# Three places a unit for side work in loops 0 and 2, and linear attention's last pieces moved into loop 2

## The chip, the cores and the metric

One core of a Trainium2 chip. The metric is the device time of the program in microseconds, the median of several runs. The profile is of one execution, and times inside it count from the start of its span.

## The reference, cut to what matters

x has 4 x 1024 tokens of 128 numbers, float32.

```python
x = x + 0.5 * ffn0(layernorm(x))          # token-shift mix: sigmoid(r) * (relu(k)**2 @ W_v)
x = x + attention(layernorm(x))           # rotary softmax attention, 16 heads of 8
x = x + 0.5 * ffn0(layernorm(x))
x = x + 0.5 * moe(layernorm(x))           # 8 experts, top 2, rms_norm inside, plus skip
x = x + linear_attention(layernorm(x))    # softplus q and k, causal, 16 heads
x = x + 0.5 * moe(layernorm(x))

def moe(x):
    xn = rms_norm(x, norm_scale)
    scores_topk, idx = top_k(xn @ w_router.T, 2)
    weights = softmax(scores_topk)
    u, gate = split(moe_linear(xn, idx, w_up))     # row i gets the weights of its expert
    down = moe_linear(u * silu(gate), idx, w_down)
    return sum(down * weights) + x
```

## The kernel before, in words

The tokens stand in 32 tiles of 128, in 8 groups of four tiles. Each of the two moe layers is computed in two halves of 16 tiles: a *round* r is one half of one layer (rounds 0 and 1 are the first layer, 2 and 3 the second). A round has a *route* and a *loop*. The route normalises the tokens, computes the router's scores, picks the top two experts, counts how many tokens each expert has, gives every copy of a token a slot in a table ordered by expert in HBM, and scatters the tokens into it (32 indirect transfers by GpSimd). The loop then goes over the 39 tiles of the table, two tiles to a unit, 20 units (`UNITS`) and three more steps for the pipeline to drain. Loop r+1 gathers the results of loop r by 32 indirect transfers.

The order of the stages is: start, attention, loop 0, loop 1, linear attention, loop 2, loop 3, and a last gather. Route 0 lies in attention, route 1 in attention and loop 0, route 2 in linear attention, route 3 in linear attention and loop 2.

In a loop, unit u on TensorE is: `turn(u)` (transpose the two gathered tiles, L1656, behind two loads of the expert's offset into a register), `up(u-1)` (L1666), `turn_hidden(u-2)` (L1678), `down(u-3)` (L1692). VectorE scales what `turn` gave (L1733) and multiplies the two halves of the hidden layer (`hidden`, L1740); ScalarE does silu (L1767) and two copies out of PSUM (L1773, L1780); SP loads the slots three units ahead (L1829) and stores the results (L1835). SP does not begin the loads of a loop before all 32 scatters of its route have landed.

Everything that isn't the loop itself is cut into *pieces*. A piece is a tuple such as `("rext", r, g)`; every engine goes through the same list and issues what it has in that piece, so that the piece's place in the list is its place in every engine's in-order queue. `plan_loop` (L457) gives every unit two places: the first between `turn` and `up`, the second between `up` and `turn_hidden`. At each place `turn_of` (L184) takes one piece from each of up to four works, but at most one piece that needs TensorE. The side pieces of a loop share PSUM bank 1.

The pieces that matter here:

- `div`, `turn`, `proj`, `stats` end the last half of attention's batch 3: each needs the piece before it (TensorE, then VectorE, then TensorE). `factors` and `mn` to `ms` are the last group of the second token-shift mix. `mt`, `mk`, `mr`, `mv` use TensorE; `md` is GpSimd alone, `mx` VectorE alone; `ms` is the statistics of the result.
- `rroot` (L1447 and the helper at L561) is 16 small VectorE instructions, one behind the other, that give the inverse roots for the tiles named; `rnorm` (L1463) one VectorE instruction per tile; `rext` (L597 by its helper) four transposes on TensorE that wait for `rnorm` of that group, and a copy by ScalarE (L1566); `rscore` (L1417) eight small matmuls and a copy (L1470).
- `rtop` (L1479 to L1489) is VectorE alone, twice; `rcount` is two matmuls (L1426, L1427) and VectorE; `rscan`, `rplace`, `roff` are VectorE alone; `rweight` ScalarE and VectorE. From `rplace` on the slots are known and the scatters (`scat`, L1601 on GpSimd) can start: one at each place, and all that are left at the last place of the last unit. GpSimd holds a scatter back until TensorE has reached the same place of the loop (`pool_follow`, L1797), as far as the loop has matmuls there.
- In linear attention the steps n run from 0 to 131. Each has a list `extra` for route pieces, taken from `routes`, a list in which `spread` (L258) leaves empty steps. `ldiv`, `lturn`, `lproj`, `lstats` end a group of it, again one behind the other, as in attention. Those of the last group, 7, are `k.l_left` (L449): every engine does them behind the last step, before loop 2.

## Time and profile before

| what | value |
|---|---|
| three runs | 1348.8, 1349.03, 1354.61 us; median 1349.03 |
| the profiled execution | 1345.49 us, its span 1343.5 us |
| busy in the span | TensorE 81%, ScalarE 60%, VectorE 49%, GpSimd 28% |
| chain that ended last | TensorE 53%, VectorE 20%, ScalarE 11%, issue 6%, GpSimd 3%, DMA 2% |
| mean granted clock of TensorE | 0.899 |

How to read it: PE is TensorE's matmuls, PEld its weight loads, DVE is VectorE, ACT ScalarE, POOL GpSimd, SPq SP's DMA queue. L1656 is line 1656 of the kernel. A granted clock of 1.00 is 2.4 GHz and one of 0.50 is 1.2 GHz; values between are means over a stretch with both. "issue" is time in which an engine waited for nothing that the profile shows. Loop 0 runs from 662.6 to about 757 us, loop 1 from 770.7 to about 850, linear attention to 1129, its last pieces to 1137, loop 2 to 1219.5, loop 3 from 1222.3 to 1293, the last gather to the end.

### The profile page before, as it was taken

The numbers are of one execution on the slowest core, as the hardware profiler recorded it, in microseconds if no ns is written. First come the engines' busy times: TensorE is split into PE (matmuls) and PEld (weight loads), VectorE is DVE, ScalarE is ACT, GpSimd is POOL, SyncE is SP. The second block draws the span as 40 slices with busy tenths as digits, with TensorE's granted clock in tenths as the row PEclk, the third lists the DMA queues.
The fourth block names the chain that finished last, engine by engine and source line by source line (L and its number), as shares of the span: only waits on it lengthen the run. The fifth ranks groups of instructions, "written<-read, shape, count | busy, mean of one in ns | idle before, by whom it ended". The sixth has DMA issues, their size and how long they took to land.

```text
span 1343.5 us, 20969 instructions
## 1 busy us (share of the span) xinstructions
PE 1084.8 (81%) x7616; PEld 504.0 (38%) x7616; DVE 657.9 (49%) x2060; ACT 807.0 (60%) x1164; POOL 376.6 (28%) x376
## 2 busy tenths in 40 slices
PE   3459899899999999999879399787887776898940
PEld 2332222222322321232256256444544344565630
DVE  5752554456355340433165157667666663633522
ACT  4328788688898899989735255644443331464520
POOL 2100111111110102333003643243331263155535
PEclk8679999899999999999999789889888686898975
DMA  4360450432036502100012233100000001143522
GB/s 139 57 96 1 65 90 1 71 57 27 1 56 96 155 1 76 54 15 30 13 40 85 81 87 93 31 17 17 12 14 1 15 33 38 50 118 99 141 66 66
DMA packets 83411, 74.07 MB, mean 55 GB/s; under 512 B 11248, under 2 KB 77680, under 8 KB 82416
## 3 DMA queue, kind: packets, MB, share of 16 engines
q1 hardware_dynamic: 73824, 55.06, 18.8%
q0 software_dynamic: 8192, 16.79, 4.3%
q8 instruction: 66, 1.08, 0.4%
q10 hardware_dynamic: 1296, 0.86, 0.2%
q14 instruction: 33, 0.27, 0.1%
HBM read 39.26 MB, written 33.42 MB: 54 GB/s over the span
## 4 chain that ended last, share of the span: by engine, by line
PE 53%; DVE 20%; ACT 11%; issue 6%; POOL 3%; DMA 2%; another core or an unknown queue 0%; SPq 0%; POOLq 0%; DVEq 0%; ACTq 0%
PE ps L994 11%; PE ps L1666 9%; ACT attn_probs L1257 8%; PE ps L979 6%; PE ps L1692 4%; PE ps L597 3%; PE ps L888 2%; PE ps L1969 2%; POOL moe_back L1611 2%; PE ps L1678 2%; PE ps L1893 1%; DVE lin_scores L2098 1%; PE ps L1656 1%; DVE stats L554 1%; PE ps L1982 1%
## 5 line engine op out<-in xcount | busy, mean ns | idle before, releaser
L1257 ACT ACTIVATE attn_probs<-ps 128x1024 f32<-128x1024 f32 x512 | 485.7, 1075 | 86.0 <-PE ps L979 85.8
L994 PE MATMUL ps<-attn_probs,attn_v 128*18 128x512 f32 x2048 | 273.9, 607 | 5.7 <-DVE room L1224 5.1
L979 PE MATMUL ps<-stack 50*128 50x512 bf16 x1024 | 167.1, 391 | 17.3 <-DMA stack<-row_maxima 11.4
L1601 POOL DMA_INDIRECT slots<-moe_xr,moe_slot x128 | 125.3, 979 | 196.3 <-ACT attn_probs L1257 81.1
L1611 POOL DMA_INDIRECT moe_back<-results,moe_slot x128 | 123.9, 968 | 110.7 <-PE ps L1656 46.8
L1666 PE MATMUL ps<-stack,lin_scores 128*128 x312 | 153.8, 616 | 0.0
L979 PEld LDWEIGHTS ps<-stack 50*128 50x128 bf16 x1024 | 34.1, 94 | 253.6 <-ACT attn_probs L1257 226.3
L1767 ACT ACTIVATE lin_scores<-ps 128x256 f32<-128x256 f32 x156 | 58.6, 382 | 107.0 <-PE ps L1666 101.8
L1740 DVE TENSOR_TENSOR lin_scores<-ps,lin_scores 128x256 f32<-128x256 f32 x156 | 59.0, 418 | 103.5 <-ACT lin_scores L1767 85.2
L1692 PE MATMUL ps<-stack,lin_scores 128*128 x624 | 85.6, 281 | 8.9 <-ACT lin_heads_out L1780 6.8
L1692 PEld LDWEIGHTS ps<-stack,lin_scores 128*128 128x128 f32 x624 | 77.7, 195 | 10.7 <-issue 10.5
L1295 POOL TENSOR_TENSOR room<-room 128x512 f32<-128x512 f32 x16 | 24.5, 1530 | 186.2 <-DVE room L1089 186.2
L1666 PEld LDWEIGHTS ps<-stack,lin_scores 128*128 128x128 f32 x312 | 55.6, 199 | 39.8 <-issue 39.8
L2098 DVE TENSOR_TENSOR lin_scores<-ps,c_causal 128x512 f32<-128x512 f32 x64 | 41.1, 683 | 49.5 <-PE ps L1969 46.8
L1733 DVE TENSOR_SCALAR lin_scores<-ps,c_norm_scale 128x256 f32<-128x256 f32 x80 | 37.8, 473 | 54.1 <-PE ps L1656 48.5
L994 PEld LDWEIGHTS ps<-attn_probs,attn_v 128*18 128x18 f32 x2048 | 34.9, 96 | 75.9 <-issue 46.8
L1089 DVE SCALAR_TENSOR_TENSOR room<-ps,c_attn_b,moe_xr 128x512 f32<-128x512 f32 x32 | 23.9, 748 | 79.9 <-PE ps L888 78.4
L2168 ACT ACTIVATE lin_scores<-ps 128x512 f32<-128x512 f32 x64 | 34.8, 594 | 45.8 <-PE ps L1969 45.5
L1656 PE MATMUL ps<-c_ident,moe_gathered 128*128 128x128 f32 x156 | 33.0, 294 | 30.7 <-DMA moe_gathered<-slots 18.7
L1773 ACT ACTIVATE lin_scores<-ps 128x512 f32<-128x512 f32 x80 | 46.8, 584 | 14.9 <-PE ps L1678 8.4
L1678 PEld LDWEIGHTS ps<-c_ident,lin_scores 128*128 128x128 f32 x312 | 39.0, 143 | 37.5 <-issue 36.3
L888 PE MATMUL ps<-room,c_qk_w 128*128 128x256 f32 x128 | 45.3, 458 | 9.2 <-DVE mix_xt L804 8.8
(237 smaller groups left out, 1567.6 us busy)
## 6 DMA issues: line engine op xcount, KB each, us to landing
stack<-qk_parts SPq DMA_DIRECT2D x48, 256.0 KB, 8.9
moe_gathered<-slots SPq DMA_DIRECT2D x76, 128.0 KB
results<-lin_heads_out SPq DMA_DIRECT2D x76, 128.0 KB
slots<-zeros SPq DMA_DIRECT2D x2, 2496.0 KB, 14.9
qk_parts<-moe_xr SPq DMA_DIRECT2D x32, 128.0 KB, 2.7
qk_parts<-moe_xr SPq DMA_DIRECT2D x16, 192.0 KB, 2.8
stack<-in_expert_w SPq DMA_DIRECT2D x1, 3072.0 KB
x<-in_x SPq DMA_DIRECT2D x8, 256.0 KB, 8.2
```

Of the source, the lines that this page charges most:

```text
L888: instruction = T.matmul(k.ps[:, bank, cols], w[:, 2 * qk + which, :], d.xt[:, half * BANK:(half + 1) * BANK][:, cols], start=True, stop=True)
L979: instruction = T.matmul(k.ps[:, SCORE_BANKS[i % 3][s], :], d.stack[b % 2][rows, 1, pair, kt * P:(kt + 1) * P], d.stack[b % 2][rows, 0, pa ...
L994: instruction = T.matmul(k.ps[32 * j:32 * j + STRIP, PV_BANK, :], d.v[:, b % 2, kt, first:first + STRIP], d.probs[:, n % A_PROBS, j * BANK ...
L1257: A.activation(d.probs[:, n % A_PROBS, 2 * e * BANK:2 * (e + 1) * BANK], k.ps[:, banks[0]:banks[1] + 1, :].rearrange("p a n -> p (a n)"), ...
L1601: G.indirect_dma_start(out=k.dram["slots"][half], out_offset=bass.IndirectOffsetOnAxis(ap=d.slot[:, s, at, c:c + 1], axis=0), in_=d.xr[:, ...
L1611: G.indirect_dma_start(out=k.back[:, at % RING, c, :], out_offset=None, in_=k.dram["results"][half], in_offset=bass.IndirectOffsetOnAxis(a ...
L1666: T.matmul(k.ps[:, bank, :], d.gt[:, u % NB, i, :], w[:, bass.ds(offset[u, i], 2 * HIDDEN)], start=True, stop=True).then_inc(k.full[bank], 1)
L1678: instruction = T.transpose(k.ps[:, bank, at:at + P], d.h[:, u % NB, i, c * P:(c + 1) * P], k.ident[:, :])
L1692: instruction = T.matmul(k.ps[:, bank, i * DIM:(i + 1) * DIM], d.ht[:, u % NB, i, c * P:(c + 1) * P], w[:, 2 * HIDDEN + c * DIM:][:, bass. ...
L1740: V.tensor_tensor(d.h[:, u % NB, i, :], k.ps[:, bank, 0:HIDDEN], d.silu[:, u % NB, i, :], ALU.mult).then_inc(k.free[bank], 1)
L1767: A.activation(d.silu[:, u % NB, i, :], k.ps[:, bank, HIDDEN:2 * HIDDEN], ACT_FN.Silu).then_inc(k.e_silu, 1)
L2098: V.tensor_tensor(d.scores[:, m % NS, :].rearrange("p (j t) -> p j t", j=HPG), k.ps[:, bank, :].rearrange("p (j t) -> p j t", j=HPG), caus ...
```

## The change

1. `plan_loop` gives each unit of loops 0 and 2 a third place, between `turn_hidden` and `down`. TensorE and ScalarE have it there; VectorE, SP and GpSimd run it right behind the second. Scatters are still put at the first and second place alone.
2. The route of round 1's second part (and of round 3's) is no longer one work of eight tiles. Group 2 is a work of its own (`route_group`), which in loop 0 begins behind `proj` and in linear attention is put into `routes` behind `lstats` of group 6. Group 3 and what follows it come behind `ms` (behind `lstats` of group 7), with an empty piece behind each `rnorm`, `rtop` and `rcount` (`spaced`).
3. `k.l_left` is not done before loop 2 any more: it is the first work of loop 2.

```diff
-    yield OTHER, ("rnorm", r, part)
+    yield OTHER, ("rnorm", r, part * TPB, (part + 1) * TPB)
...
+def route_group(r, g):
+
+    yield OTHER, ("rroot", r, g * TPG, (g + 1) * TPG)
+    yield OTHER, ("rnorm", r, g * TPG, (g + 1) * TPG)
+    yield PRODUCT, ("rext", r, g)
+    yield PRODUCT, ("rscore", r, g)
...
+def spaced(pieces):
+
+    out = []
+    for piece in pieces:
+        out += [piece] + [(OTHER, ("rest",))] * (piece[1][0] in ("rnorm", "rtop", "rcount"))
+    return out
...
+        if ("lstats", GROUPS - 2) in out:
+            routes += spread(route_group(3, HALF_GROUPS - 2))
...
-    k.l_left = [piece for work in works for _, piece in work] + scatters
-    fill(k.l_left)
+    assert not scatters
+    k.l_left = works
...
-    slots = [[] for _ in range(2 * (UNITS + 3))]
+    places = [[[] for _ in range(PLACES)] for _ in range(UNITS + 3)]
+    slots = [place for unit in places for place in unit[:2]]
...
-        works = [list(route_part(3, 1, TPB)) + list(route_slots(3))]
+        works = k.l_left
...
+    for n, out in enumerate(place for unit in places for place in unit) if r % 2 == 0 else ():
+        out += turn_of(works, 4)
+        if n % PLACES < 2:
+            out += scatters if n // PLACES == UNITS + 2 and n % PLACES else scatters[:1]
+            scatters = scatters[1:]
+        if ("stats", BATCH - 1, HALVES - 1) in out:
+            works.insert(0, [(OTHER, ("factors", TILES - TPG, TILES))] + list(side_mix(SIDE_MIXES - 1)))
+        if ("proj", BATCH - 1, HALVES - 1) in out:
+            works.append(list(route_group(1, HALF_GROUPS - 2)))
+        if ("ms", SIDE_MIXES - 1) in out:
+            assert not works
+            works.append(spaced(route_group(1, HALF_GROUPS - 1)) + spaced(route_slots(1)))
+        if ("lstats", GROUPS - 1) in out:
+            works.append(spaced(route_group(3, HALF_GROUPS - 1)) + spaced(route_slots(3)))
+        if ("rplace", r + 1) in out:
+            scatters = transfers("scat", r + 1)
...
@@ -1695,7 +1722,7 @@
-        first, second = k.e_plan[r][u]
+        first, second, third = k.e_plan[r][u]
...
@@ -1709,6 +1736,8 @@
             side(piece)
         if 0 <= u - 2 < UNITS:
             turn_hidden(u - 2)
+        for piece in third:
+            side(piece)
         if 0 <= u - 3 < UNITS:
             down(u - 3)
...
-        for piece in second:
+        for piece in second + third:
             side(piece)
...
-    for piece in k.l_left:
-        side(piece)
-        route(piece)
```

## Rows read from the trace of the kernel before

**Rows 1.** Stretches: length, busy PE, PEld, DVE, ACT, POOL; PEclk, DMA share, GB/s

```profile
755.20:770.70 15.50, 0.01 (x1) 0.00 (x0) 0.00 (x0) 0.28 (x1) 9.83 (x11) 0.50 0.21 65
...
770.70:776.40 5.70, 4.98 (x10) 2.44 (x11) 0.96 (x2) 0.56 (x2) 3.79 (x4) 0.50 0.48 135
...
679.50:684.00 4.50, 4.50 (x21) 2.95 (x21) 1.21 (x4) 1.75 (x4) 0.24 (x1) 0.75 0.21 58
...
695.00:700.80 5.80, 3.18 (x18) 1.99 (x16) 5.32 (x30) 1.86 (x5) 0.00 (x0) 1.00 0.33 91
...
1116.00:1119.40 3.40, 0.00 (x0) 0.00 (x0) 0.20 (x1) 0.60 (x1) 2.92 (x4) 0.89 0.15 49
...
1119.40:1125.00 5.60, 5.05 (x42) 3.47 (x42) 1.84 (x4) 1.40 (x3) 3.08 (x4) 0.50 0.11 38
...
1170.00:1210.00 40.00, 39.15 (x215) 26.87 (x214) 14.68 (x36) 24.01 (x59) 24.00 (x25) 1.00 0.39 113
```

**Rows 2.** Timeline, end of loop 0 (start, length, engine, what, idle before it)

```profile
747.39 0.96 POOL L1601 DMA_INDIRECT slots<-moe_xr,moe_slot  x1 [0.42 <-PE ps L1666]
...
756.99 0.28 ACT L1780 ACTIVATE lin_heads_out<-ps 128x128 f32<-128x128 f32 x1 [3.13 <-remote]
...
766.36 0.96 POOL L1601 DMA_INDIRECT slots<-moe_xr,moe_slot  x1 [0.30 <-issue]
...
768.60 3.21 SPq L1829 DMA_DIRECT2D moe_gathered<-slots  x5
```

**Rows 3.** TensorE's waits from 663 to 751 us (total, times, longest)

```profile
PE ps L597 <- DVE moe_xr L1463: 2.6, 1, 2.6
...
PE ps L597 <- DVE room L586: 2.3, 1, 2.3
...
PE ps L1426 <- DVE moe_both L1488: 1.7, 1, 1.7
...
PE ps L771 <- DVE mix_mixed_r L811: 1.1, 1, 1.1
```

**Rows 4.** Timeline, from linear attention into loop 2

```profile
1134.32 2.08 PE L1942 MATMUL ps<-c_lin_w,stack 128*128 128x128 f32 x8 [0.69 <-ACT stack L2150]
...
1144.15 1.12 PE L597 MATMUL ps<-c_ident,moe_xr 128*128 128x128 f32 x4 [3.19 <-DVE moe_xr L1463]
...
1145.06 3.62 PE L1666 MATMUL ps<-stack,lin_scores 128*128 x4
...
1152.44 0.95 PE L1417 MATMUL ps<-router_scaled,moe_xrt 128*128 128x8 f32 x8
...
1153.94 1.88 PE L1666 MATMUL ps<-stack,lin_scores 128*128 x4
...
1159.10 0.23 PE L1426 MATMUL ps<-moe_both,before_bf 128*128 128x128 bf16 x1 [1.73 <-DVE moe_both L1488]
```

**Rows 5.** Timeline, TensorE, two expert matmul groups one unit apart

```profile
1177.13 1.88 PE L1666 MATMUL ps<-stack,lin_scores 128*128 x4
...
1180.39 1.88 PE L1666 MATMUL ps<-stack,lin_scores 128*128 x4
```

**Rows 6.** Timeline, loop 0: its first matmuls and VectorE's side pieces

```profile
667.37 1.88 PE L1666 MATMUL ps<-stack,lin_scores 128*128 x4
...
667.57 0.69 DVE L1157 TENSOR_TENSOR x<-x,ps 128x512 f32<-128x512 f32 x1 [0.41 <-PE ps L946]
...
694.49 0.86 DVE L554 BATCH_NORM_STATS2 stats<-x 128x6 f32<-128x128 f32 x4
...
696.05 0.16 DVE L1452 TENSOR_SCALAR moe_root_var<-moments 128x8 f32<-128x8 f32 x1
...
698.97 0.75 DVE L1740 TENSOR_TENSOR lin_scores<-ps,lin_scores 128x256 f32<-128x256 f32 x2
...
699.64 2.13 DVE L1463 TENSOR_SCALAR moe_xr<-x,moments,moe_root 128x128 f32<-128x128 f32 x8
...
701.69 0.47 DVE L1733 TENSOR_SCALAR lin_scores<-ps,c_norm_scale 128x256 f32<-128x256 f32 x1
```

More of the change, by code:

```diff
@@ L1711, in pe_loop @@
             turn_hidden(u - 2)
+        for piece in third:
+            side(piece)
         if 0 <= u - 3 < UNITS:
@@ L1743, in dve_loop @@
     for u in range(UNITS + 3):
-        first, second = k.e_plan[r][u]
+        first, second, third = k.e_plan[r][u]
         if u < UNITS:
@@ L1792, in act_loop @@
             turn_hidden(u - 2)
+        for piece in third:
+            side(piece)
         if 0 <= u - 3 < UNITS:
@@ L1853, in sp_loop @@
             store(u - 3)
-        for piece in second:
+        for piece in second + third:
             side(piece)
@@ L2222, in pool_linear @@
             route(piece)
-    for piece in k.l_left:
-        side(piece)
-        route(piece)
 class Stage:
```

35 lines of the change are left out of this document (10 added, 25 removed).

## The prediction

> **What bounds the kernel now.** I read the chain that ended last, then the busy time by stretch, then the timeline where a stretch is thin. The chain is mostly TensorE, with a share for VectorE (the shares stand in the table of the profile), so I ask where TensorE stands still around the changed places. There are three. (a) After loop 0 it has nothing for 15.5 us, 755.2 to 770.7 [rows 1]. The timeline shows why [rows 2]: GpSimd issues scatters back to back, from 747.39 to 766.36, 16 of them, 18.97 / 15 = 1.265 us apart; the last ends at 767.32, SP's load of loop 1 starts 1.28 us later, TensorE 2.1 us behind that. ScalarE had finished loop 0 at 757.27. The scatters set the end of (a), not the loop. (b) In loop 0, pieces make TensorE wait for VectorE: 2.6, 2.3, 1.7 and 1.1 us [rows 3], 7.7 us together, and the clock is 0.75 over the 4.5 us behind the second of them [rows 1], some 1.1 us of full speed lost. (c) Between linear attention and loop 2 the chain of group 7 (ldiv, lturn, lproj) ends on TensorE at 1136.4, and the first expert matmuls start at 1145.06 [rows 4], since `rext` waits for VectorE's `rroot` and `rnorm` of eight tiles.
>
> **The scatters.** The positions follow from the generators. Before, `rplace` of route 1 lies in unit 12's first place; 20 scatters follow one by one and 12 pile up in the last place of unit 22. After: div 0.0, turn 0.1, proj 0.2; rest and rroot(group 2) 1.0; stats and rnorm 1.1; factors and rext 1.2; mn and rscore 2.0; mt 2.1, md 2.2, mx 3.0, mk 3.1, mr 3.2, mv 4.0, ms 4.1; rroot(group 3) 4.2, rnorm 5.0, rest, rext 5.2, rscore 6.0, rtop 6.1 and 7.0, rcount 7.2, rscan 8.1, rplace 8.2. Scatters run from 9.0, two per unit (2.53 us of GpSimd in a unit of 3.26 us, [rows 5]), and 5 are left for the last place. The last scatter that waits for the loop is that of 20.1 both times, and it is followed by 15 before (the row at 747.39 is it) and by 8 after. 7 x 1.265 = **8.9 us** off the gap. What is late next: ScalarE and SP end the loop at 757.3, so with the loads at 768.6 - 8.9 = 759.7 about 2 us are left until the loop's own end decides. TensorE still stands some 7 us there, longer than the 3.4 us of 1116.0 to 1119.4, behind which the clock was 0.50 [rows 1]; the restart stays at the lower level and I take no gain in it.
>
> **Loop 0's body.** All work of the pieces is kept, so only waits and clock count. Removed: the 7.7 us of waits and the 1.1 us of clock above. Added, by following TensorE and VectorE in order:
> rext(group 2) at 1.2 stands behind up(0), whose last matmul is issued at about 669.1 (667.37 + 1.88, less 0.2 of overlap with the next; [rows 6]). VectorE must by then have done the proj add (till about 667.9; before at 667.57 + 0.69, [rows 6]), turn(1) 0.5, rroot 2.9 (696.05 to 698.97; its cost is per instruction, so a half of the tiles costs the same), hidden(0) 0.75, stats 1.25, rnorm of four tiles 1.1 (half of 2.13) [rows 6]: 674.4. Wait: 5.3 us. The proj, which now has no turn(1) ahead of it, waits 0.8 for its copy (0.69, the copy being of the add's size). mk at 3.1 waits about 0.6 (VectorE does turn(3) 0.5 and the two mx after GpSimd's difference). rext(group 3) at 5.2: between ms and it VectorE has stats 1.25, rroot 2.9, turn(5) 0.5, rnorm 1.1, begun about 2 us after mv; TensorE has th, down, turn, up, th, some 4 us: it waits 3.2 us, where before it waited 2.6. rcount with its empty place waits no more. Sum added: 9.9 us of waits against 7.7.
> The clock: a wait of 5.3 us is longer than that stand of 3.4 too; back at work on loop matmuls it needs about 6 us (0.50 over 770.7 to 776.4, 4.98 us busy) [rows 1], so 2.5 us are lost; behind the 3.2 us wait the same may happen or not (over 695.0 to 700.8, with a 2.6 us wait in it, it stayed 1.00): I take 0.8, bounds 0 and 2.5. So loop 0's body is (9.9 - 7.7) + (3.3 - 1.1) = **4.4 us longer**. Bounds: no clock loss and a first wait hidden down to the 2.6 us of the old one, 4.9 us better; both stretches at the low level in full and 2 us more waiting, 4 us worse.
> The Trainium skill (TensorE: Matmul & The Clock Gate, Part 1) says that the warm-up is a budget of time and not a number of matmuls. By that rule each of the two waits would cost the same 2.5 us, 1.7 more than my sum; the row with clock 1.00 behind the 2.6 us wait speaks for a smaller second one.
>
> **VectorE and GpSimd.** Four rroots in place of two: 2.9 us more of VectorE in loop 0 and as much in linear attention. Priced in the waits above in loop 0; in linear attention it falls at steps 121 to 123, where TensorE stands 3.4 us anyway [rows 1]: nothing. If that stand went, up to 2.9 us would show. GpSimd's proj additions lie ahead of the first scatter and hold nothing up; SP gets no new piece, its stores come ahead of the second and third places as before.
>
> **Linear attention into loop 2.** Two pieces, rext and rscore of group 6, move into steps 126 and 128, on the path: 1.12 us for the turn [rows 4] and about 1.8 for the scores (0.95 at full clock [rows 4], the level there being 0.50 [rows 1]): +2.9. turn(0) now goes ahead of ldiv, +0.4. So lproj ends at 1136.4 + 3.3 = 1139.7 (2.08 us of it from 1134.32, [rows 4]). Then turn(1) and up(0) at once, the latter 3.6 at the low level [rows 4], till 1143.5: the first expert work stands 5 us ahead of before. But rext(group 3) at 2.2 waits: silu 0.5, hidden 0.75, stats 1.25, rroot 2.9, turn(2) 0.5, rnorm 1.1 bring VectorE to 1150.6, TensorE having run out (up(1), th(0)) at about 1146.5. Then turn(3), rscore, and up(2) starts at 1153.0 at full clock, 1154.2 at the low level, against 1153.94 before [rows 4]. At the low level 1.3 more is lost behind it. The rcount wait of 1.73 [rows 4] goes. Together between -2.6 and -0.1; after 4 us of standing I take the latter: **0.1 us**. Scatters of route 3 end one later behind the loop's last paced one (1.265 us); the last store and load hide it.
>
> **The sum.** -8.9 + 4.4 - 0.1 = -4.6 us. The profiled execution took 1345.5 us around a span of 1343.5, so 1340.9 for it; it is 3.5 below the median of the runs shown, 1349.0, to which the same difference gives **1344.4 us**.
>
> **The rivals.** *The new waits are cheap.* If the clock keeps its higher level behind the 3.2 and the 4 us waits (as over 695.0 to 700.8), and some of VectorE's work slips into gaps that my order does not see, loop 0's body is even or 1 us longer and loop 2 brings 2.6: -8.9 + 1 - 2.6 = -10.5, 1338.5 us. For it: the change's empty places are cut just for that. Against: the first wait has no empty place. *The waits take all.* Both low stretches in full (+1.7), 2 us more of waiting at the first, and a late instruction stretch such as that at 1116.0 once more, some 1 us: about 1349, no change. *Slower: the clock stays low.* Over 1119.4 to 1125.0 TensorE was busy 5.05 of 5.6 us and still had 0.50 [rows 1], so being busy does not by itself bring it back. If from the first wait (674.4) it stayed at that level for the seven units that still hold pieces, 7 x 3.26 = 23 us of work at full speed would take 23 us more, less 3.8 of the later waits that vanish and 3.3 counted: +15.9, so 1360.3. It decides at the first expert matmuls behind rext(group 2): clock 0.5 beyond 6 us. The Trainium skill (same page, Part 4, PE-mode transpose) states that transposes do not count as busy in the same way; by that rule the pieces, of which rext and mt are transposes, would favour this case. Against it: the steady loop, whose every unit has two sets of transposes, is granted the full clock, 1.00 over 1170 to 1210 [rows 1]. *No effect in place:* VectorE runs the third place right behind the second, so for it only the spacing changes; where its work ends last, as in both first waits, the third place gives nothing. That is inside the forecast.
>
> **How the numbers follow.** Forecast (-2 to -6.7) 0.45; cheap waits 0.35; the waits take all 0.12; slower 0.08. The range holds the forecast, the no-change case and most of the cheap one: 1336 to 1350. A measurement of this kernel tells about 0.5%, 6.7 us, from no change. Faster by more than that: the cheap case with a little of the forecast's edge, 0.38; within it 0.54; slower 0.08.
>
> **What would show it.** Right: 8 scatters behind the last that waits for TensorE in loop 0, the load of loop 1 1.3 us behind them; a wait of TensorE for `moe_xr` of about 5 us near 670 to 674 and one of about 3 near 697; a clock near 0.5 for some us behind the first; loop 2's first expert matmuls about 5 us earlier, and a wait of about 4 us two units on. Wrong: no such waits (cheap case), or loop 0's last scatters hidden behind its own end (then less than 8.9 is to be had), or units at half clock till unit 7.

## The result, and the profile after

| kernel | median, us | ratio to before |
|---|---|---|
| before, 20 runs | 1348.91 (1343.91 to 1354.61) | |
| after, 20 runs | 1352.95 (1349.22 to 1356.52) | 1.0030, 95% 1.0019 to 1.0041 |

The change makes the kernel 4.0 us slower (1352.95 - 1348.91). The forecast was 1344.4 in 1336 to 1350: the loss is small, inside the 0.5% named there, but the time lies outside the range and on the other side of before.

**Loop 0's waits** came as the prediction had them, but for two. TensorE's waits from 659 to 751 us in the trace of after, where before had [rows 3] (waited for, us in total, times, longest):

```profile
PE ps L624 <- DVE moe_xr L1490: 8.6, 2, 5.4
...
PE ps L798 <- DVE mix_mixed_r L838: 1.7, 1, 1.7
PE ps L1453 <- DVE moe_both L1515: 1.7, 1, 1.7
...
PE ps L1683 <- DVE lin_scores L1762: 0.9, 1, 0.9
PE ps L973 <- DVE room L1179: 0.9, 1, 0.9
```

The 8.6 us are rext(group 2), 5.4 where 5.3 was forecast, and rext(group 3), 3.2. mk waits 1.7 instead of 0.6, and rcount still 1.7 instead of nothing.

**The gap behind loop 0**, against [rows 2], in the timeline of after (start, busy time, engine, line, what; idle time before it and what ended it):

```profile
755.47 0.95 POOL L1628 DMA_INDIRECT slots<-moe_xr,moe_slot  x1 [0.42 <-PE ps L1693]
...
758.72 0.38 ACT L1809 ACTIVATE lin_heads_out<-ps 128x256 f32<-128x256 f32 x1 [2.27 <-remote]
...
760.87 0.38 ACT L1802 ACTIVATE lin_scores<-ps 128x256 f32<-128x256 f32 x1 [1.76 <-issue]
...
765.14 0.38 ACT L1809 ACTIVATE lin_heads_out<-ps 128x256 f32<-128x256 f32 x1 [3.88 <-remote]
765.57 0.95 POOL L1628 DMA_INDIRECT slots<-moe_xr,moe_slot  x1 [0.30 <-issue]
...
765.66 1.22 PE L1719 MATMUL ps<-stack,lin_scores 128*128 x4 [5.26 <-issue]
...
768.71 0.28 ACT L1809 ACTIVATE lin_heads_out<-ps 128x128 f32<-128x128 f32 x1 [3.19 <-remote]
769.44 3.24 SPq L1860 DMA_DIRECT2D moe_gathered<-slots  x5
...
771.60 0.69 PE L1683 MATMUL ps<-c_ident,moe_gathered 128*128 128x128 f32 x2 [4.73 <-DMA moe_gathered<-slots]
```

Eight scatters behind one that is paced by TensorE, as counted; the last ends at 766.52. But the load comes at 769.44, not 1.3 us behind it: ScalarE's last copy of the loop ends at 768.99. From the paced scatter to that copy it is 13.5 us, against 9.9 (747.39 to 757.27) before [rows 2]. TensorE and ScalarE stand in this tail for 1.8 to 5.3 us at a time, marked "remote" or "issue": the trace names no instruction of this core for which they wait.

**From linear attention to loop 2**, against [rows 4], the timeline of TensorE after:

```profile
1139.06 2.05 PE L1973 MATMUL ps<-c_lin_w,stack 128*128 128x128 f32 x8 [0.78 <-ACT stack L2175]
...
1141.32 2.96 PE L1693 MATMUL ps<-stack,lin_scores 128*128 x4
...
1144.34 1.88 PE L1693 MATMUL ps<-stack,lin_scores 128*128 x4
...
1151.11 1.12 PE L624 MATMUL ps<-c_ident,moe_xr 128*128 128x128 f32 x4 [4.45 <-DVE moe_xr L1490]
...
1153.01 1.85 PE L1444 MATMUL ps<-router_scaled,moe_xrt 128*128 128x8 f32 x8
...
1154.71 3.76 PE L1693 MATMUL ps<-stack,lin_scores 128*128 x4
...
1160.92 1.88 PE L1693 MATMUL ps<-stack,lin_scores 128*128 x4
...
1163.89 0.23 PE L1453 MATMUL ps<-moe_both,before_bf 128*128 128x128 bf16 x1 [0.65 <-DVE moe_both L1515]
...
1166.03 0.41 PE L1683 MATMUL ps<-c_ident,moe_gathered 128*128 128x128 f32 x2 [0.78 <-issue]
```

The first expert matmuls start at 1141.32 instead of 1145.06. Five us later TensorE waits 4.45 us for `rnorm` of group 3, as worked out, and is then at the lower clock for ten us. The rows from 1160.92 on come behind that: up(3), `rcount`, which waits 0.65 us (1.73 before), and the next `turn`. Of the next rows the upper is the stretch behind loop 0's first wait, the lower the one behind 1151.11 (stretch, busy PE, PEld, DVE, ACT, POOL; PEclk, DMA share, GB/s):

```profile
675.00:679.00 4.00, 4.00 (x11) 2.45 (x12) 1.56 (x6) 0.38 (x1) 0.00 (x0) 0.50 0.11 33
1151.10:1161.00 9.90, 9.61 (x33) 6.86 (x34) 3.24 (x11) 2.06 (x5) 0.00 (x0) 0.52 0.00 0
```

Landmarks of all traces that follow, read off their timelines. Loop 0 counts from its first `turn`: the last `up`, the last copy by ScalarE, the end of the last scatter, the first `turn` of loop 1. The rest counts from linear attention's first copy of its sums: the last such copy, loop 2's first and last `up`, loop 3's first `turn`.

| trace | up(19) | copy | scatter | loop 1 | lin. end | up(0) | up(19) | loop 3 |
|---|---|---|---|---|---|---|---|---|
| before | 83.5 | 94.7 | 104.8 | 108.2 | 261.3 | 277.1 | 345.1 | 354.3 |
| after | 95.0 | 109.8 | 107.3 | 112.4 | 264.8 | 272.4 | 349.3 | 360.4 |
| after_again | 92.6 | 98.3 | 105.0 | 108.4 | 259.3 | 265.7 | 340.8 | 349.3 |
| loop0_only | 92.8 | 98.5 | 105.2 | 108.7 | 252.4 | 265.9 | 331.7 | 340.2 |
| loop2_only | 84.0 | 89.7 | 105.2 | 108.7 | 259.5 | 265.9 | 341.1 | 349.6 |
| loop0_only_2 | 94.0 | 105.9 | 106.4 | 110.0 | 261.3 | 277.1 | 344.9 | 354.1 |
| loop2_only_2 | 85.0 | 96.9 | 106.2 | 109.5 | 261.7 | 269.7 | 346.3 | 357.0 |

One thing is needed to read it. The kernels ran on several chips, in sessions of two kinds: before takes 1344 to 1349 us in those of the first kind and 1329 to 1331 in those of the second. The first two and the last two rows are from the first kind, the three between from the second. A ratio is always to before in the same session; it is estimated over all runs and differs a little from the ratio of the medians. What makes the kind is not known: the expectations speak of chips, but the chip numbered 6 stands in both kinds (before at 1329.9 in one session, at 1348.5 in another), and whether that is the same chip is not on record. Of before there is a trace of the first kind alone; for the second, the half of loop0_only and of loop2_only that is left as it was stands for it.

### The profile page after: what moved, and what is told of

Same layout as the page of the kernel before. It is cut to its first block, busy times and chain, and to the rows that moved or that the text cites. A ratio compares the mean times of both kernels' runs of the same rounds, so it can differ in the third digit from the quotient of the medians.

```text
span 1351.1 us, 20959 instructions
## 1 busy us (share of the span) xinstructions
PE 1081.6 (80%) x7573; PEld 509.4 (38%) x7616; DVE 664.2 (49%) x2092; ACT 806.6 (60%) x1164; POOL 376.0 (28%) x376
## 4 chain that ended last, share of the span: by engine, by line
PE 51%; DVE 20%; ACT 12%; issue 5%; POOL 3%; another core or an unknown queue 2%; DMA 2%; SPq 0%; POOLq 0%; DVEq 0%; ACTq 0%
PE ps L1021 11%; ACT attn_probs L1284 8%; PE ps L1693 8%; PE ps L1006 6%; PE ps L1719 4%; PE ps L624 3%; PE ps L915 2%; POOL moe_back L1638 2%; PE ps L2000 2%; PE ps L1705 2%; PE ps L1683 1%; PE ps L1924 1%; DVE lin_scores L2126 1%; PE ps L1960 1%
## 5 line engine op out<-in xcount | busy, mean ns | idle before, releaser
L1693 PE MATMUL ps<-stack,lin_scores 128*128 x312 | 157.6, 629 | 0.0
L1719 PE MATMUL ps<-stack,lin_scores 128*128 x624 | 85.9, 281 | 13.5 <-issue 9.9
L915 PE MATMUL ps<-room,c_qk_w 128*128 128x256 f32 x128 | 43.6, 441 | 11.2 <-DVE mix_xt L831 8.8
L1809 ACT ACTIVATE lin_heads_out<-ps 128x256 f32<-128x256 f32 x80 | 30.2, 377 | 37.3 <-PE ps L1719 24.7
```

The costliest lines, as they stand in the source:

```text
L915: instruction = T.matmul(k.ps[:, bank, cols], w[:, 2 * qk + which, :], d.xt[:, half * BANK:(half + 1) * BANK][:, cols], start=True, stop=True)
L1693: T.matmul(k.ps[:, bank, :], d.gt[:, u % NB, i, :], w[:, bass.ds(offset[u, i], 2 * HIDDEN)], start=True, stop=True).then_inc(k.full[bank], 1)
L1719: instruction = T.matmul(k.ps[:, bank, i * DIM:(i + 1) * DIM], d.ht[:, u % NB, i, c * P:(c + 1) * P], w[:, 2 * HIDDEN + c * DIM:][:, bass. ...
```

## Experiments

### Which half loses the time

`loop0_only` takes the change in loop 0 alone, `loop2_only` that in linear attention and loop 2 alone, `after_again` both.

```diff
 loop0_only: loop 2's works and k.l_left as before
-        works = k.l_left
+        works = [list(route_part(3, 1, TPB)) + list(route_slots(3))]
...
 loop2_only: loop 0's works as before, at the first two places
-            works.append(spaced(route_group(1, HALF_GROUPS - 1)) + spaced(route_slots(1)))
+            works.append(list(route_part(1, 1, TPB)) + list(route_slots(1)))
...
```

> The change in loop 0 alone; linear attention, its last pieces and loop 2 are as before. Theory A (the traces of before and after add up: in loop 0 the body grew by 11.5 us and the gap behind it shrank by 7.2, in linear attention and loop 2 another 6 us were lost): this one is 0 to 4 us slower than before, 1349 to 1353 us, and the part between the first turn of loop 0 and the first of loop 1 is 112 us instead of 108. Theory B (all of the loss is loop 0's, loop 2's part gives some back): 5 to 7 us slower, 1354 to 1356. My prediction on record had -4.5, 1344.4.

> The other half alone: loop 0 as before; group 6 of route 3 in linear attention, the last pieces in loop 2 with three places. Theory A: 3 to 6 us slower than before, 1352 to 1355: linear attention ends 3.5 us later, and the first expert matmuls of loop 2 come 4 us earlier but a wait of 4 to 5 us for moe_xr with a half clock behind it takes that back. Theory B: 1 to 3 us faster, 1346 to 1348. My prediction on record had -0.1, 1348.9.

> The changed kernel unchanged, to see which stalls of its trace come back. If the late signals of TensorE at 1180 to 1182.5 (three engines wait for it together) and in loop 0's tail (ScalarE late by 2.3, 1.8, 3.9 and 3.2 us) belong to the kernel, they stand at the same instructions again, to 0.5 us. If they belong to one execution, they are somewhere else. Time 1352 to 1354.

Measured, with before at 1329.1: loop0_only 1332.1, 1.0015 (0.9994 to 1.0036); loop2_only 1339.9, 1.0079 (1.0054 to 1.0104); after_again 1341.3, 1.0079 (1.0049 to 1.0108). In a session with before at 1344.5 the two halves were run again:

> The same kernel as loop0_only. On a chip with before at 1330 it was 1.0015 of it: a body 8.6 us longer and a gap 8.9 us shorter. On a chip with before at 1349 the tail of the loop was 11.2 us long in the trace of before and 14.8 in that of after, against 5.7 there, and decides the gap. Theory T (this tail takes the gain of the scatters): 4 to 7 us over before there, 1.003 to 1.005. Theory N (the long tail of after was one execution): 0 to 2 us over, 1.000 to 1.002.

> The same kernel as loop2_only: 1.0079 of before on a chip with before at 1330, where linear attention runs at the full clock up to its end. On a chip with before at 1349 the trace of before has a stand of 3.4 us and the lower clock behind it at that place, so that the added wait and the clock behind it cost little. Theory T: 0 to 3 us over before there, below 1.002. Theory N: 1.005 to 1.008 on either.

loop0_only_2 1345.5, 1.0002 (0.9988 to 1.0016); loop2_only_2 1349.2, 1.0032 (1.0016 to 1.0047).

So on both kinds the loss is that of linear attention and loop 2, and loop 0's half is not told from no change. Theory A's 3 to 6 us for loop 2's half fit the first kind (4.3, from the ratio 1.0032) and are too low for the second (10.5, from 1.0079); its 112 us for loop 0 did not come. B fell. Of the second pair of expectations N was right for loop 0: the long tail does not cost it its gain. For loop 2's half 1.0032 lies between T and N. The traces agree: loop 0 with its gap takes 108.4 and 108.7 with the change, 108.7 without (after_again, loop0_only, loop2_only); from the first copy of the sums to loop 3 it is 349.3 and 349.6 with the change and 340.2 without, 9.3 us. In the session of loop2_only_2 that is 357.0 against 354.1, 2.9 us.

after_again does not show the stalls in loop 0's tail: its last copy is 5.7 us behind the last `up`, as in all traces of the second kind (5.6 or 5.7), where the paced kernels of the first have 11.1 to 14.8, before among them; `hold_tail`, below, has 6.3. Nor does it show the late signals at 1182.5, which come back in loop2_only_2, of the first kind (4.9 us from up(8) to up(9), 3.3 in after_again). They go with the kind of session.

### What loop 2's half loses

In the trace of loop0_only, loop 2 starts as before, without the stand of [rows 1] at 1116.0. What linear attention calls groups 6 and 7 are groups 2 and 3 of round 3. TensorE's timeline in loop0_only:

```profile
1126.03 0.44 PE L1680 MATMUL ps<-c_ident,moe_gathered 128*128 128x128 f32 x2 [1.39 <-DMA moe_gathered<-slots]
1128.54 0.66 PE L1680 MATMUL ps<-c_ident,moe_gathered 128*128 128x128 f32 x2 [2.07 <-DVE lin_scores L1759]
1132.39 1.12 PE L621 MATMUL ps<-c_ident,moe_xr 128*128 128x128 f32 x4 [3.20 <-DVE moe_xr L1487]
```

and in after_again, with the windows of its two low stretches there (columns as above):

```profile
1115.62 1.11 PE L624 MATMUL ps<-c_ident,moe_xr 128*128 128x128 f32 x4 [1.92 <-DVE moe_xr L1490]
...
1124.03 0.69 PE L1683 MATMUL ps<-c_ident,moe_gathered 128*128 128x128 f32 x2 [0.20 <-DMA moe_gathered<-slots]
...
1130.35 2.91 PE L1693 MATMUL ps<-stack,lin_scores 128*128 x4
...
1140.08 1.11 PE L624 MATMUL ps<-c_ident,moe_xr 128*128 128x128 f32 x4 [4.44 <-DVE moe_xr L1490]
...
1143.67 3.76 PE L1693 MATMUL ps<-stack,lin_scores 128*128 x4
```

```profile
1115.60:1125.00 9.40, 9.18 (x75) 7.19 (x76) 2.60 (x8) 1.79 (x3) 3.46 (x4) 0.50 0.26 81
1139.40:1149.40 10.00, 9.01 (x29) 6.29 (x30) 3.41 (x12) 1.96 (x4) 0.00 (x0) 0.50 0.01 2
```

Three things are seen. The moved `rext` of group 6 waits 1.92 us for VectorE, and behind it TensorE has the clock 0.50 for 9.4 us, with 9.18 busy: linear attention ends 6.9 us later than in loop0_only (259.3 - 252.4). Loop 2's first `turn` waits for its load in both, which SP issues when route 2's scatters have landed (in loop0_only the last ends at 1122.66, the load is issued at 1123.93); up(0) is at 265.7 and 265.9. And rext(group 3) waits 4.44 us, with ten us at 0.50 behind it; loop 2 takes 75.1 us from its first to its last `up` instead of 65.8.

Where those 9.3 us lie is told by the starts of single `up`s, counted as in the table above:

| trace | up(2) | up(3) | up(4) | up(9) | up(19) |
|---|---|---|---|---|---|
| before | 285.9 | 291.2 | 294.6 | 312.4 | 345.1 |
| after | 285.8 | 292.0 | 297.3 | 317.0 | 349.3 |
| loop0_only | 273.9 | 279.1 | 282.5 | 299.3 | 331.7 |
| after_again | 279.0 | 285.2 | 290.5 | 308.4 | 340.8 |
| warm (below) | 278.7 | 283.4 | 289.8 | 307.7 | 340.0 |

Up to up(2) after_again has lost 5.2 us against loop0_only; on the first kind the earlier start pays for that, and after is level with before. Behind up(2) both lose about 4 us more (4.2 and 4.0). Of these 0.9 come up to up(3), with the clock low. 2.0 come up to up(4), where the clock is back at 1.00 and where `rcount` now lies: in before it waits 1.73 us ahead of up(3), in after 0.65 us ahead of up(4), and the `turn` behind it stands another 0.78 (the rows at 1163.89 and 1166.03 above). The unit with `rcount` in it takes 5.4 us in after and 5.3 in before, so nothing was saved there. The last 1.1 to 1.4 are smaller stands in the units behind.

`warm` keeps TensorE busy in the four waits for `rext`, with matmuls into the bank that the rext overwrites:

```diff
+            for _ in range({(1, 2): 5, (1, 3): 3, (3, 2): 2, (3, 3): 4}.get((r, g), 0)):
+                bank, n = k.use[piece]
+                T.wait_ge(k.free[bank], n)
+                T.matmul(k.ps[:, bank, :], k.ident[:, :], k.expert_w.rearrange("p e c -> p (e c)")[:, 0:4 * P],
+                         start=True, stop=True)
             T.wait_ge(k.e_xr, HALF_GROUPS * r + g + 1)
```

> The changed kernel, with 5, 3, 2 and 4 idle matmuls of 128x512 (0.94 us each) ahead of the four rext that wait for VectorE (5.2, 3.1, 1.9 and 4.4 us), into the PSUM bank that the rext then overwrites; the output is the same. The waits stay, only TensorE is not idle in them. Theory C (half of the loss is the clock behind the waits: in the trace of after it is 0.50 over the 9.4 us behind the rext in linear attention and some 10 us behind the one in loop 2, and 0.57 to 0.66 over 10 us in loop 0, some 13 us lost at the lower level): 9 to 13 us less than after, about the time of before or up to 3 us below it. Theory W (the waits themselves are the loss, the clock comes back as late either way, or falls for another reason): within 2 us of after, that is 0.6 to 0.8% over before.

Measured 1335.3, 1.0041 (1.0022 to 1.0060), with before at 1329.9: 5 us less than after_again (0.0038 x 1330). Its windows, and three rows of TensorE in loop 2:

```profile
672.00:682.00 10.00, 7.93 (x37) 4.45 (x35) 8.08 (x37) 2.22 (x5) 0.74 (x1) 1.00 0.04 13
1113.00:1120.00 7.00, 6.23 (x75) 4.25 (x70) 4.54 (x17) 1.18 (x2) 5.40 (x6) 1.00 0.15 49
1120.00:1130.00 10.00, 5.87 (x47) 5.10 (x36) 1.03 (x3) 2.48 (x3) 0.00 (x0) 0.59 0.24 72
1137.00:1145.00 8.00, 6.21 (x23) 3.43 (x22) 4.19 (x18) 0.60 (x1) 0.00 (x0) 0.84 0.01 2
```

```profile
1123.20 0.69 PE L1688 MATMUL ps<-c_ident,moe_gathered 128*128 128x128 f32 x2 [2.58 <-DMA moe_gathered<-slots]
...
1140.18 0.66 PE L624 MATMUL ps<-c_ident,moe_xr 128*128 128x128 f32 x4 [1.01 <-DVE moe_xr L1495]
...
1151.72 0.23 PE L1458 MATMUL ps<-moe_both,before_bf 128*128 128x128 bf16 x1 [1.71 <-DVE moe_both L1520]
```

The clock stays 1.00 through loop 0's waits and to the end of linear attention. Then loop 2's first `turn` waits 2.6 us for its load, which the earlier end had uncovered, and the clock goes all the same. So theory C is right in kind, the clock behind the waits costs time, but 5 us and not 9 to 13. And most of the 5 us are not where the change loses: loop 0 with its gap takes 105.2 us instead of 108.4, and from the first copy of the sums to loop 3 it is 348.5 instead of 349.3. In loop 2 up(3) follows up(2) after 4.8 us instead of 6.2, the clock being higher, but then `rcount` waits 1.71 us for VectorE's `moe_both` instead of 0.67, and up(4) follows after 6.4 us instead of 5.3. There the gain of the clock is handed on to the next wait for VectorE. (One trace each.)

`group6_loop2` does group 6 in loop 2, at unit 0.0 and 1.1:

```diff
-        if ("lstats", GROUPS - 2) in out:
-            routes += spread(route_group(3, HALF_GROUPS - 2))
-        works = k.l_left
+        works = k.l_left + [rested(route_group(3, HALF_GROUPS - 2), 2)]
```

> The changed kernel, but group 6 of route 3 is not done inside linear attention: its rroot lies at unit 0.0 of loop 2, its rext at 1.1. Theory L (moving it into linear attention costs 6.9 us: a wait of 1.9, the turn and the scores, and the lower clock for the 9.4 us behind it): linear attention ends 6.9 us earlier; loop 2 gets a wait of 2 to 4 us more at unit 1 and takes some of it back: 2 to 5 us less than after. Theory 0 (it falls into time in which TensorE stands anyway, as my prediction has it): no less than after, or 2 to 4 us more for what loop 2 has to do in addition.

Measured 1340.0, 1.0082 (1.0051 to 1.0114). Linear attention is 7 us shorter and nothing is gained:

```profile
1124.91 0.69 PE L1689 MATMUL ps<-c_ident,moe_gathered 128*128 128x128 f32 x2 [6.42 <-DMA moe_gathered<-slots]
...
1125.87 1.76 PE L1966 MATMUL ps<-c_head_rows,lin_sums 128*128 128x36 f32 x8
...
1132.53 2.60 PE L1699 MATMUL ps<-stack,lin_scores 128*128 x4
```

`turn(0)` now stands 6.42 us ahead of the last pieces of linear attention, which need nothing from it. Theory L had the 6.9 us right and missed where they go. That is a fact that my prediction lacked: **loop 2 cannot start before route 2's scatters are through**. On the second kind, where linear attention ends sooner, a few us saved or lost on TensorE before that are hidden behind them: turn(0) comes at 258.6, 259.4 and 258.6 in loop0_only, after_again and group6_loop2. In the traces of before and after it does not wait for its load: it comes at 268.2 and 264.8, 10.5 and 5.8 us behind SP's issue.

`no_second_root` leaves the added inverse roots out (14 VectorE instructions, twice; the roots of an earlier round serve instead):

```diff
+            if (r, piece[2]) not in ((1, 2 * TPG), (3, 2 * TPG)):
                 V.tensor_scalar(var[:, 0, :], moments[:, :, 1], LN_EPS, None, ALU.add)
...
```

> The changed kernel without the inverse roots of group 2 in round 1 and of group 6 in round 3 (the 14 small VectorE instructions of the added rroot; its last two, the keep factors, stay); the roots of an earlier round are used for these tiles, so that the routing differs. Theory V (VectorE is what TensorE waits for at all these points, and the second rroot of 2.9 us is the added work): each of the two gets 2.5 us shorter, the wait of 5.2 us in loop 0 falls to 2.7 and that of 1.9 in linear attention goes, with some of the clock behind them: 3 to 8 us less than after, 0.2 to 0.5% over before. Theory P (the places are wrong, a wait of this length is hidden or taken by the next one): within 2 us of after, 0.6 to 0.8% over before.

Measured 1340.7, 1.0068 (1.0043 to 1.0092), against 1.0079 of after_again: not told apart. The wait of 5.2 us became 4.3, that of 4.4 stayed, that of 1.9 in linear attention went, with its low clock, and `turn(0)` waits 4.9 us for the load instead. VectorE now waits 1.69 us for ScalarE's silu. The chain from `proj` through the unit to `rnorm` is long even without the roots. Theory V's 3 to 8 us did not come in the traces (0.7 us less in loop 0, 0.3 more behind it), as P has it; the intervals alone do not rule out 3.

`rests` puts more empty places behind three rnorm: 4 for group 2 in loop 0 and 3 for the last group in loop 2 (`rested` does it), and three empty steps for group 6 in linear attention (not shown):

```diff
-            works.append(list(route_group(1, HALF_GROUPS - 2)))
+            works.append(rested(route_group(1, HALF_GROUPS - 2), 4))
...
-            works.append(spaced(route_group(3, HALF_GROUPS - 1)) + spaced(route_slots(3)))
+            works.append(rested(route_group(3, HALF_GROUPS - 1), 4) + spaced(route_slots(3)))
```

> The changed kernel with empty places in front of the rext that wait: 4 more in loop 0 for group 2, three steps in linear attention for group 6, 3 more in loop 2 for group 3. The waits of 5.2, 1.9 and 4.4 us should go, that of 3.1 stays; loop 2's scatters come one unit later (two more behind its end, 2.5 us, hidden or not). Theory W+C (waits and the clock behind them are the whole loss): 5.2 + 1.9 + 4.4 = 11.5 us of waits and some 10 of clock, less 8 for work of VectorE that still has to be waited for elsewhere (before had 3.2 + 2.1 us at this point in loop 2, and 2.4 in loop 0): 8 to 14 us less than after, 0 to 4 us below before. Theory D (VectorE has too much to do there, every piece only passes its wait to the next): less than 3 us below after.

Measured 1336.3, 1.0042 (1.0024 to 1.0060), 5 us below after_again, less than the 8 to 14 of theory W+C. The three waits went. In their place `mt` in loop 0 waits 7.0 us for VectorE (2.4 in loop2_only), and `turn` in loop 2 3.5 us for VectorE's scaling of the unit before. Here too the gain is loop 0's: 105.3 us with its gap. Loop 2's last `up` comes 2.6 us sooner than in after_again (338.2), but loop 3 only 0.4 (348.9), for its load again waits for scatters, which now end later. As theory D has it, part of a wait is passed on: VectorE has its 4 us of `rroot` and `rnorm` to do in the first units, and every engine's queue is in order.

### Other arrangements

`one_part` has one rroot of eight tiles in loop 0 (with three places), and of group 6 only VectorE's part in linear attention; `one_part_unpaced` also lets the scatters run free:

```diff
 one_part, loop 0
-            works.append(spaced(route_group(1, HALF_GROUPS - 1)) + spaced(route_slots(1)))
+            works.append(rested(route_part(1, 1, TPB), 2) + spaced(route_slots(1)))
...
 one_part_unpaced
-                if piece[0] in ("gath", "scat"):
+                if piece[0] == "gath":
                     pool_follow(G, k, r, u, second)
```

> Three places a unit as in the changed kernel, but in loop 0 the route of round 1 has one rroot and one rnorm of eight tiles again, with two empty places behind; scatters start at unit 10 instead of 9 (12 before). Linear attention's last pieces are done before loop 2 again; of group 6 only rroot and rnorm (VectorE alone) lie in linear attention, its rext is loop 2's first piece, and group 7's rroot comes at unit 1. If my reading of the losses is right (loop 0: the second rroot makes the body longer; linear attention: the turn, the scores and the clock behind them on TensorE; loop 2: the wait of 4.4 us and the clock behind it): loop 0's body is 2 to 4 us longer than before instead of 8.6 and the gap 6.3 shorter, 2 to 4 us gained; the first expert matmuls of loop 2 start some 5 us earlier than before and 3 to 4 us of that are kept: 4 to 8 us below before. If the third place or the order in itself costs: no better than before.

> The kernel one_part, and GpSimd issues the scatters without holding each back until TensorE is at its place. If the last scatters set the gap behind loop 0 there (10 behind the last paced one, 11.4 us): back to back they end some 3 us earlier, and the gap is shorter by that until the loop's own end decides: 2 to 4 us below one_part. If back-to-back scatters beside the loop slow it (their DMA traffic, or late signals as in the tail of the trace of after), it is not below one_part.

Measured: one_part 1331.1, 1.0004 (0.9982 to 1.0025); one_part_unpaced 1324.5, **0.9946** (0.9923 to 0.9968), with before at 1331.1. one_part is no faster, where 4 to 8 us were expected: it starts loop 2's experts 2.9 us earlier than loop0_only (263.0 against 265.9) and has lost 4.7 by its last `up`; loop 0 with its gap is 107.5, against 108.7. Earlier starts are again given back in the next units. Without the pacing loop 0 takes 102.6.

`loop0_one_part` is loop 0 of one_part with the rest as before:

> Loop 0 as in one_part (three places, one rroot of eight tiles, scatters from unit 10, held back as before), linear attention and loop 2 as before. In the trace of one_part loop 0 with its gap took 107.5 us against 108.2 to 108.7 with loop 0 as before, and the rest is before's: 1 us below before, 0.999, within the interval of no change on either kind of chip. If the loss of loop 0's second rroot is larger than the traces show: 0.996 to 0.998. If the long tail of a chip with before at 1345 takes the gain (10 scatters instead of 15 beside it, the tail at 11 us): 1.000 to 1.001.

1344.2, 0.9989 (0.9970 to 1.0007), with before at 1345.5: no difference that can be told.

### What scatters do to the engines beside them

`after_unpaced`, `before_unpaced` and `best` (loop 0 of one_part_unpaced, the rest as before) take the pacing away as above; `hold_tail` does the opposite in the kernel before:

```diff
+                if piece[0] == "scat" and u > UNITS:
+                    bank, n = k.use["edown", r, UNITS - 1]
+                    G.wait_ge(k.free[bank], n + 1)
```

> The changed kernel, but GpSimd does not hold a scatter back until TensorE is at the same place: 32 scatters run back to back from 719.8, 40.5 us, to 760.3, instead of 766.5. Theory 1 (scatters running back to back beside the draining loop are what makes its tail slow: 13.5 us from the last paced scatter to the last copy, 9.9 before): only some four lie in the tail, it is 4 to 7 us shorter, loads of loop 1 at 762 to 765, in loop 2 a few us as well: 1343 to 1348. Theory 2 (the tail is slow by itself): loads stay at 769, time as after, 1352 to 1354. Theory 3 (back-to-back scatters slow TensorE's signals wherever they run): the units from 9 on get longer, more than 3.3 us each, and it is slower than after, 1355 to 1360.

1335.4, 1.0036 (1.0016 to 1.0057), before at 1329.1: 6 us less than after_again, the amount of theory 1. The reason of theory 1 is not seen: the tail is 5.7 us in both, the scatters end 40.1 us behind the start of the first, and loop 1 starts 2.6 us earlier (105.8 against 108.4); the rest is not located in the two traces.

> The kernel before, and GpSimd issues the scatters of loops 0 and 2 without holding each back until TensorE is at its place; nothing else is changed. In the trace of before they start at 723.4 and end at 767.3, 43.9 us for 32; back to back they need 40.5. If the scatters alone set the gap behind loop 0: 3.4 us less, and loop 2, whose scatters end before its last copy, gains nothing: 3 to 4 us below before, ratio 0.997. If what helps in the unpaced kernels is something else (places in which GpSimd's wait holds back others), more than that; if the traffic of unpaced scatters slows the loop, 0 to 3 us above before.

> Loop 0 as in one_part_unpaced (three places, one rroot of eight tiles, scatters from unit 10, not held back), linear attention and loop 2 as before. The part from the first turn of loop 0 to that of loop 1 was 102.6 us in one_part_unpaced and 108.2 before: 5.6 us gained; the part from linear attention's first copy of the sums to loop 3 was 342.7 there and 340.2 with loop 2 as before: another 2.5 us. Sum: 8 us below before, ratio 0.994; at least as fast as one_part_unpaced (0.9946). If loop 2's part of one_part_unpaced is no loss (the two traces are one execution each), it is 0.9946 to 0.997.

> The same kernel as before_unpaced, once more. Theory S (scatters that are not held back delay TensorE's signals to the other engines, 4 to 10 us each in the trace of before_unpaced, but only on some chips: those on which before takes 1349, not those on which it takes 1330): on a chip with before at 1349 again 1.03 to 1.04 of it, on one with before at 1330 it is 0.997 to 1.000. Theory K (it is this kernel's own, whatever the chip): 1.03 to 1.04 on either.

before_unpaced 1397.2, **1.0360** (1.0332 to 1.0388), best 1405.0, **1.0424** (1.0402 to 1.0446), both with before at 1348.5; before_unpaced_2 1395.9, 1.0390 (1.0360 to 1.0421), before at 1344.5. I had expected 0.994 to 1.003 for the first two; of the third, S and K both had 1.03 to 1.04 in a session of this kind, so it does not tell them apart. ScalarE's waits from 726 to 768 us, beside the scatters, in before_unpaced, and in one_part_unpaced with before at 1331:

```profile
ACT lin_scores L1773 <- remote: 13.7, 2, 10.1
ACT lin_heads_out L1780 <- remote: 12.9, 2, 9.9
ACT lin_scores L1767 <- remote: 9.7, 2, 5.1
```

```profile
ACT lin_scores L1802 <- PE ps L1699: 5.6, 9, 1.2
ACT lin_heads_out L1815 <- PE ps L1725: 4.8, 12, 1.1
```

and what that leaves of 34 us beside 28 scatters, first before_unpaced, then one_part_unpaced:

```profile
727.00:761.00 34.00, 10.59 (x41) 5.77 (x39) 1.99 (x5) 4.47 (x11) 25.77 (x28) 0.69 0.21 67
```

```profile
727.00:761.00 34.00, 30.42 (x171) 21.25 (x171) 10.21 (x25) 21.19 (x55) 25.77 (x28) 1.00 0.39 115
```

The scatters are the same, 28 with 25.77 us of GpSimd; TensorE gets 10.6 us of matmuls done in the one, 30.4 in the other. The longest stands of TensorE and VectorE in loop 0 of before_unpaced:

```profile
757.91 1.12 PE L1678 MATMUL ps<-c_ident,lin_scores 128*128 128x128 f32 x4 [15.58 <-issue]
...
767.82 0.48 DVE L1733 TENSOR_SCALAR lin_scores<-ps,c_norm_scale 128x256 f32<-128x256 f32 x1 [19.88 <-remote]
```

Expected of hold_tail:

> The kernel before, but the 15 scatters behind that of 20.1 in loop 0 (and the few in loop 2) are held back until ScalarE's last copy of the loop. No scatter runs beside the draining loop. Theory S: the tail, from the last up to the last copy, is 5.7 us and not 11.2, on any chip; the gap behind it is 15 scatters long, so that the whole is 0 to 4 us slower than before. Theory I (late instructions of ScalarE and TensorE, whatever GpSimd does): the tail is 9 to 12 us on a chip with before at 1349, and the whole 5 to 8 us slower.

1355.0, 1.0068 (1.0044 to 1.0092), before at 1344.5. With no scatter beside the draining loop, ScalarE's last copies come as TensorE's matmuls end:

```profile
749.87 0.38 ACT L1780 ACTIVATE lin_heads_out<-ps 128x256 f32<-128x256 f32 x1 [0.97 <-PE ps L1692]
...
751.58 0.38 ACT L1780 ACTIVATE lin_heads_out<-ps 128x256 f32<-128x256 f32 x1 [1.05 <-PE ps L1692]
752.85 0.28 ACT L1780 ACTIVATE lin_heads_out<-ps 128x128 f32<-128x128 f32 x1 [0.88 <-PE ps L1692]
```

The last copy ends 5.0 us behind the paced scatter at 748.11, against 9.9 before [rows 2] and 13.5 after, and 6.3 us behind the last `up`. So theory S holds for the tail: the scatters issued back to back make it long, in sessions of the first kind (11.2 us before, 6.3 here). The whole is 9 us slower (0.0068 x 1344.5), more than the 0 to 4 expected. In the trace loop 0 with its gap is 4.8 us longer (113.0 against 108.2), since 15 scatters then follow; the rest lies behind it and is not explained: linear attention ends 3.7 us later (265.0) and loop 2's tail is 1.8 longer. What delays TensorE's signals was not tried; that it goes with the kind of session is shown only by one_part_unpaced and after_unpaced against the three others, and no unpaced kernel ran on both kinds.

## Why the prediction was wrong, point by point

**The scatters, -8.9 us.** Right, by the traces of the second kind. Eight follow the paced one, and without the long tail the gap is 15.8 us (108.4 - 92.6) instead of 24.7 (108.7 - 84.0). In the trace of the result the tail decides, which I had given 2 us of slack: I took its end from the trace of before, where it was already stretched, and let it move with the body alone. Over the 12 runs of loop0_only_2 this costs nothing that can be told (1.0002).

**Loop 0's body, +4.4 us.** Mis-sized: 8.6 (92.6 - 84.0). Waits at 5.2, 0.9 and 3.1 stand where 5.3, 0.8 and 3.2 were worked out (the 3.2 by luck: its terms add up to 3.75). The term "rcount with its empty place waits no more" is wrong, it waits 1.7; mk waits 1.7 for 0.6; two small ones, 0.9 and 0.3, were not seen. Up to up(19) TensorE stands 17.2 of 92.6 us in after_again and 11.2 of 84.0 in loop2_only: 6.0 more, where the sum had 2.2. It is busy 2.6 us longer (75.4 against 72.8), where the sum had 2.2 for the clock. So -8.9 and +8.6: loop 0 gives nothing.

**"In linear attention it falls at steps 121 to 123, where TensorE stands 3.4 us anyway: nothing."** That stand goes with the first kind: 3.6 us of "issue" again in loop0_only_2 and hold_tail, 5.0 in loop2_only_2, absent in loop0_only. Where it is absent, the added work waits 1.9 us and the clock is 0.50 behind it, +6.9 to the end of linear attention. I had named the condition ("if that stand went, up to 2.9 us would show") and not its clock. But these 6.9 us do not reach loop 2, which waits for its load.

**The first expert matmuls 5 us earlier.** Right for the first kind, that of the result: 4.7 and 7.4 us (277.1 to 272.4 and to 269.7). Nothing on the second (265.9 to 265.7), where turn(0) waits for its load.

**"At the low level 1.3 more is lost behind it. The rcount wait of 1.73 goes", "-0.1".** This is the step that failed. The wait of 4.2 us came at 4.45, and up(2) stood at 285.8 against 285.9 before, level as forecast. From there to the last `up` after loses 4.2 us. First, the clock: from up(2) to up(3) it takes 6.2 us, 2.9 more than the steady 3.27, where I had 1.3; the low stretch lasted 9.9 us with 9.61 busy at 0.52, 4.6 us lost in all, against the 2.5 priced for it. Second, the wait of `rcount` did not go. It is 0.65 us for VectorE and 0.78 at the `turn` behind it, and the unit takes 5.4 us where before's takes 5.3, so the 1.73 that I took off did not come; the same term was wrong in loop 0. `warm` shows that the clock is not what sets this: with a higher clock behind up(2), `rcount` waits 1.71. Third, some 1.4 us of small stands up to up(9), for which I had nothing. I followed the edit to the unit where both kernels stood level and closed the sum there with a wait taken off. In after the tail adds 1.7 (8.1 against 6.4 us from the last `up` to the last copy). The whole term is +2.9 us in loop2_only_2 and +6.1 in after, by the runs +4.3 (0.0032 x 1344.5, interval 2.2 to 6.3), in place of -0.1; on the second kind, where the earlier start is missing, 9.3 in the traces.

**The clock.** The prediction had 2.5 and 0.8 us behind loop 0's two waits for `rnorm`. Three windows of after_again, behind the wait of 5.2 us, behind that of 3.1, and behind `rcount` (1.7 us, and 0.7 at the next `turn`):

```profile
671.60:678.60 7.00, 6.54 (x18) 4.11 (x19) 3.59 (x20) 0.98 (x2) 0.00 (x0) 0.51 0.06 19
697.10:705.10 8.00, 7.54 (x44) 5.51 (x45) 3.63 (x12) 3.12 (x7) 0.00 (x0) 1.00 0.16 43
709.10:714.10 5.00, 4.51 (x16) 2.71 (x17) 1.24 (x4) 1.44 (x4) 0.00 (x0) 0.66 0.21 56
```

So some 3.2 us are lost behind the first, nothing behind the second, and 1.5 behind `rcount`, where I had none; busy time times the missing share of the clock gives these. By the same count 4.6 are lost behind the 4.45 us in loop 2 and 4.6 behind the 1.92 us in linear attention (0.50 over 9.4 us). The Trainium skill (TensorE: Matmul & The Clock Gate, Part 1) says that the warm-up is a budget of time, though it also calls it run-variable; by that each wait would cost about the same, and 0 to 4.6 us is not the same. The rival by its Part 4, that units with many transposes stay low for long, did not come either: in the units that hold pieces the longest low stretch behind a wait was ten us. Why the clock comes back after 3 us in one place and after ten in another is open.

**The sum.** -8.9 + 8.6 + 4.3 = +4.0, the measured difference; that it fits to the tenth is chance, since the first two terms are single traces of the second kind and the third is runs of the first. My -4.6 was that sum with two terms 4.2 and 4.4 us too small. "The waits take all" (1349, 0.12) was the nearest rival, and had 3.7 of the first error and none of the second. "Slower" I had tied to a clock that stays low for seven units and put at 0.08. With loop 0's body at its bad bound my own sum gave -0.6; what took it to +4 is loop 2's term, for which I had given no bound above -0.1.

## What to carry to other kernels

Follow a moved wait until the two kernels have kept the same distance for two units, not to the first point at which they are level: here that was seven units further, and 4.2 us came in them. Take a wait off the sum only when the chain that ends it is shown to end sooner: an empty place moves TensorE's instruction, not the VectorE result for which it waits. Keeping the clock up, or spacing a wait out, pays only where nothing else waits next: both gave 3 us in loop 0 and less than 1 from linear attention to loop 3. Ask of every stage what its first instruction waits for when the work ahead of it is shortened; a load behind a row of scatters is a floor that no reordering on TensorE moves. A stand in one trace is not cover until it is known to be in others.

## What was not expected of the hardware

Scatters that GpSimd issues back to back (1.26 us apart) beside a loop cost nothing with before at 1329 to 1331 (one_part_unpaced, after_unpaced) and 49 to 57 us with before at 1344 to 1349 (1397.2 - 1348.5, 1395.9 - 1344.5, 1405.0 - 1348.5). There, in loop 0 of before_unpaced, ScalarE stood up to 10.1 us and VectorE 19.9 us with "remote" as the reason, and TensorE itself 15.6 us at one `turn_hidden`. The pacing that holds each scatter back to TensorE's place, with GpSimd still issuing 78% of the time (2.53 of 3.26 us), avoids it in the loop; in the tail, where before issues them back to back too, it costs some 5 us (11.2 against 6.3 in hold_tail). Whether it is the chip or something else about the session that makes the two kinds is not shown. So no version here is known to beat before on both kinds: one_part_unpaced is 0.5% faster on the one, and best, whose loop 0 is the same, 4.2% slower on the other, where one_part_unpaced itself was not run.
